# A graph layer on one core: spare products on zeros in the first unit, the weights' split moved off GpSimd, and one branch's columns copied out a unit earlier

## The reference

```python
def cxin_conv(x, a, eps, W, b):
    ax = a @ x
    h = ax + (1.0 + eps[0]) * ax
    for i in range(3):
        h = relu(h @ W[i].T + b[i])
    return h

h = maximum(layernorm(x), 0.0)
out1 = cxin_conv(h,  adj, eps1, W1, b1)
out2 = cxin_conv(x2, adj, eps2, W2, b2)
result = x + concatenate((out1, out2), axis=1) @ Wm.T + bm
```

## Time and profile before

| | |
|---|---|
| median of 3 runs | 415.06 us (414.89 to 415.40) |
| the profiled execution's own time | 414.96 us |
| its span, first to last instruction | 413.1 us |
| PE, busy | 404.5 us, 98% of the span, 1747 products |
| DVE, busy | 220.4 us, 53% |
| ACT, busy | 218.9 us, 53% |
| POOL, busy | 34.1 us, 8% |
| mean granted TensorE clock | 0.995 of full |

### The profile page before, as it was taken

One profiled execution on the slowest core, in us unless ns is written; L12 is line 12 of the kernel. 1 busy time (PEld: TensorE's weight loads), 2 busy tenths in 40 slices (PEclk: granted clock), 3 DMA queues, 4 the chain that ended last, 5 costly groups with the idle time before them and its releaser, 6 DMA issues.

```text
span 413.1 us, 4963 instructions
## 1 busy us (share of the span) xinstructions
PE 404.5 (98%) x1747; PEld 326.8 (79%) x1747; DVE 220.4 (53%) x274; ACT 218.9 (53%) x271; POOL 34.1 (8%) x37
## 2 busy tenths in 40 slices
PE   7999989999999999999999999999999999999996
PEld 2887768888888888888888888888888888888884
DVE  5899975452834456434555426455273454755222
ACT  5888892355543354553435554335554335765032
POOL 1443460000100000000100001000010000000100
PEclk9899999999999999999999999999999999999999
DMA  7998568432755508355293444843265541740100
GB/s 254 396 411 314 203 225 309 188 122 98 254 203 203 195 33 287 144 203 203 80 332 109 152 191 149 308 160 130 116 236 221 203 176 52 267 167 1 52 0 25
DMA packets 14745, 76.15 MB, mean 184 GB/s; under 512 B 2000, under 2 KB 2256, under 8 KB 6928
## 3 DMA queue, kind: packets, MB, share of 16 engines
q1 hardware_dynamic: 13392, 71.97, 46.8%
q0 software_dynamic: 1200, 3.93, 2.8%
q10 hardware_dynamic: 144, 0.13, 0.1%
HBM read 73.93 MB, written 2.10 MB: 184 GB/s over the span
## 4 chain that ended last, share of the span: by engine, by line
PE 85%; DVE 6%; ACT 5%; issue 2%; DMA 1%; SPq 1%; ACTq 0%; DVEq 0%
PE acc L429 25%; PE acc L433 25%; PE acc L430 25%; DVE adj_lo L386 3%; PE hidden L430 3%; PE hidden L429 3%; PE hidden L433 2%; ACT adj_hi L257 2%; DMA adj_raw<-adj_tiles 1%; DVE stats L354 1%; PE merged L430 1%; PE merged L429 1%; PE merged L433 1%; ACT x_rows L274 1%; DVE var_eps L359 1%
## 5 line engine op out<-in xcount | busy, mean ns | idle before, releaser
L429 PE MATMUL acc<-adj_hi,feat_lo 128*128 128x512 f32 x448 | 175.0, 391 | 1.6 <-ACT act_f L241 1.6
L433 PE MATMUL acc<-adj_lo,feat_hi 128*128 128x512 f32 x448 | 174.8, 390 | 0.0
L430 PE MATMUL acc<-adj_hi,feat_hi 128*128 128x512 f32 x448 | 174.3, 389 | 0.0
L330 DVE TENSOR_TENSOR adj_lo<-adj_raw,adj_hi 128x2048 fp32r<-128x2048 f32 x56 | 128.2, 2327 | 26.7 <-ACT adj_hi L224 26.7
L336 DVE TENSOR_TENSOR act_lo<-act_f,act_hi 128x512 fp32r<-128x512 f32 x60 | 41.4, 691 | 124.7 <-ACT act_f L241 124.7
L224 ACT ACTIVATE adj_hi<-adj_raw 128x2048 fp32r<-128x2048 f32 x56 | 104.8, 1930 | 2.2 <-PE acc L433 2.0
L429 PEld LDWEIGHTS acc<-adj_hi,feat_lo 128*128 128x128 f32 x448 | 84.1, 188 | 19.6 <-issue 2.0
L240 ACT ACTIVATE act_hi<-hidden,bias 128x512 fp32r<-128x512 f32 x45 | 31.0, 688 | 129.1 <-PE hidden L433 129.1
L433 PEld LDWEIGHTS acc<-adj_lo,feat_hi 128*128 128x128 f32 x448 | 84.1, 188 | 18.2
L430 PEld LDWEIGHTS acc<-adj_hi,feat_hi 128*128 128x128 f32 x448 | 84.1, 188 | 18.0
L240 ACT ACTIVATE act_hi<-acc,ax_scale 128x512 fp32r<-128x512 f32 x15 | 10.3, 688 | 44.7 <-PE acc L433 44.7
(11 more groups left out here) (60 smaller groups left out, 200.5 us busy)
## 6 DMA issues: line engine op xcount, KB each, us to landing
adj_raw<-adj_tiles SPq DMA_DIRECT2D x61, 1024.0 KB, 5.1
x_rows<-x_tiles SPq DMA_DIRECT2D x16, 256.0 KB, 6.4
adj_raw<-adj_tiles SPq DMA_DIRECT2D x12, 256.0 KB, 6.2
x_res<-x_t POOLq DMA_DIRECT2D x8, 256.0 KB, 6.2
out_t<-y_sb POOLq DMA_DIRECT2D x7, 256.0 KB, 2.3
w_raw<-w_t SPq DMA_DIRECT2D x1, 512.0 KB, 9.0
out_t<-y_sb SPq DMA_DIRECT2D x1, 128.0 KB, 1.8
out_t<-y_sb ACTq DMA_DIRECT2D x1, 128.0 KB, 1.9
```

Source lines behind the costliest of these rows:

```text
L330: nc.vector.tensor_tensor(adj_lo[:, u % RING, :], adj_raw[:, u % RING, :], f32(adj_hi[:, u % RING, :]), ALU.subtract).then_inc(lo_made, 1)
L429: nc.tensor.matmul(out, lhs_lo, rhs_hi, start=start, stop=False)
L430: nc.tensor.matmul(out, lhs_hi, rhs_hi, start=False, stop=False)
L433: return nc.tensor.matmul(out, lhs_hi, rhs_lo, start=False, stop=stop)
```

## The change

There are three parts. PE gets three more products on zeros at its start (`WARM_UP` 15), and two more (`FILLERS`) behind each of the four high x high products of unit 0 of branch 1. The weights are loaded three units earlier in SP's queue, split on ACT (`w_hi`, behind unit 5's features) and on DVE (`w_lo`, behind the last `adj_lo` of the first chunk), and POOL no longer touches them. The copies of step 0 are taken apart: branch 1's stand behind unit 0 of the next chunk, branch 0's behind unit 1 as before.

```diff
-    WARM_UP = 12
+    WARM_UP = 15
+    FILLERS = 2
+    WEIGHTS_AT = U - 3
-    OPERAND_AFTER = {1: 0, 3: 1, 5: 2, 7: 3}
+    OPERAND_AFTER = {0: ((0, BRANCH_ORDER[0]),), 1: ((0, BRANCH_ORDER[1]),),
+                     **{u: tuple((k, b) for b in BRANCH_ORDER) for u, k in {3: 1, 5: 2, 7: 3}.items()}}
-    LAST_OPERAND_AFTER = {1: 0, 3: 1, 4: 2, 5: 3}
+    LAST_OPERAND_AFTER = {0: ((0, BRANCH_ORDER[0]),), 1: ((0, BRANCH_ORDER[1]),),
+                          **{u: tuple((k, b) for b in BRANCH_ORDER) for u, k in {3: 1, 4: 2, 5: 3}.items()}}
...
-                if u == U - 2:
+                if u == WEIGHTS_AT - 2:
                     sp.dma_start(w_raw[:, :, :], w_t).then_inc(w_loaded, 16)
...
-            pool.wait_ge(w_loaded, 16)
-            nc.gpsimd.tensor_copy(w_hi[:, :, :], w_raw[:, :, :]).then_inc(w_hi_made, 1)
-            pool.wait_ge(w_hi_made, 1)
-            nc.gpsimd.tensor_tensor(w_lo[:, :, :], w_raw[:, :, :], f32(w_hi[:, :, :]),
-                                    ALU.subtract).then_inc(w_lo_made, 1)
             pool.dma_start(x_res[:, :], x_t[:, 0:CW]).then_inc(res_loaded, 16)
...
                 rectify(u)
+                if u == WEIGHTS_AT:
+                    act.wait_ge(w_loaded, 16)
+                    nc.scalar.activation(w_hi[:, :, :], w_raw[:, :, :], ACT.Copy).then_inc(w_hi_made, 1)
             act.wait_ge(bias_loaded, 16)
             act.wait_ge(scale_made, 1)
...
                 for j in range(JB):
                     fine_low(u, j)
+            dve.wait_ge(w_hi_made, 1)
+            nc.vector.tensor_tensor(w_lo[:, :, :], w_raw[:, :, :], f32(w_hi[:, :, :]),
+                                    ALU.subtract).then_inc(w_lo_made, 1)
             dve.wait_ge(eps_loaded, 16)
             dve.wait_ge(bias_loaded, 16)
...
+            def idle_products(n):
+                for _ in range(n):
+                    nc.tensor.matmul(merged[:, :], zeros[:, 0:P], zeros[:, :], start=True, stop=True)
...
                     nc.tensor.matmul(acc[b][:, :], feat_hi[:, b, u * JB + j, :], adj_hi[:, s, cols],
                                      start=(u == 0 and j == 0), stop=False)
+                    if fine and u == 0:
+                        idle_products(FILLERS)
```

More of the change, by code:

```diff
@@ L241, in branch_operand @@
                 nc.scalar.activation(act_f[:, b, :], src[:, :], **how).then_inc(act_f_made[b], 1)
-            def operand(m, k):
-                for b in BRANCH_ORDER:
-                    branch_operand(m, k, b)
             def fine_high(u, j):
@@ L294, in _ @@
                     high_of_unit(c, u)
-                    if u in OPERAND_AFTER:
-                        operand(c - 1, OPERAND_AFTER[u])
+                    for k, b in OPERAND_AFTER.get(u, ()):
+                        branch_operand(c - 1, k, b)
             for u in range(U):
                 high_of_unit(LAST, u)
-                if u in LAST_OPERAND_AFTER:
-                    operand(LAST - 1, LAST_OPERAND_AFTER[u])
+                for k, b in LAST_OPERAND_AFTER.get(u, ()):
+                    branch_operand(LAST - 1, k, b)
             for k in range(STEPS):
@@ L337, in low_of_branch @@
                                         ALU.subtract).then_inc(act_lo_made[b], 1)
-            def low_of_operand(m, k):
-                for b in BRANCH_ORDER:
-                    low_of_branch(m, k, b)
             def result(m):
@@ L402, in _ @@
                     low_of_unit(c, u)
-                    if u in OPERAND_AFTER:
-                        low_of_operand(c - 1, OPERAND_AFTER[u])
+                    for k, b in OPERAND_AFTER.get(u, ()):
+                        low_of_branch(c - 1, k, b)
                 result(c - 1)
@@ L407, in _ @@
                 low_of_unit(LAST, u)
-                if u in LAST_OPERAND_AFTER:
-                    low_of_operand(LAST - 1, LAST_OPERAND_AFTER[u])
+                for k, b in LAST_OPERAND_AFTER.get(u, ()):
+                    low_of_branch(LAST - 1, k, b)
             result(LAST - 1)
@@ L536, in _ @@
             pe.wait_ge(zeros_made, 1)
-            for _ in range(WARM_UP):
-                nc.tensor.matmul(merged[:, :], zeros[:, 0:P], zeros[:, :], start=True, stop=True)
+            idle_products(WARM_UP)
             for u in range(U):
```

## The result

The changed kernel takes 416.92 us (416.50 to 418.92, 6 runs), against 415.19 us in the same comparison: 1.0042 of the time before, 95% interval 1.0027 to 1.0057. It is 1.7 us slower. The forecast was 416.15 with a range up to 416.7, so the direction was right and the range too short by 0.2 us.

The account below looks back on a forecast made before the run. Feeding engines, through ACT's chain, bound the time before 58 us, PE's products the rest. Products on zeros 0, weights with earlier copies +1.15, on 414.96: 416.1, or 416.15 by the median; range 414.8 to 416.7.

Parts of the forecast that it names:

- Part 1, the products on zeros: Unit 0 on PE: up to 1.6 us sooner or 2.7 later, absorbed by the feeders before 58 us; 0.
- Part 2, the weights: First chunk's end: `w_lo` delays POOL and `ax_scale`, so ACT's loop and the third product; +1.15 us with the earlier copies.
- its cover: ACT's 0.91 us idle for `var_eps` absorbs `w_hi`; bounds 0 to 0.25 us, taken as 0.
- POOL ahead of DVE's next instruction: Behind `w_lo`, waiting POOL runs `feat_lo` first, to about 54.7; `ax_scale` ends at 54.75 instead of 52.40.
- Part 3, the earlier copies: Start of chunk 1: a gain of 1.1 us, taken by the late `ax_scale`; later chunks 0.
- The sum's +1.15: Chunk 1's third product at 59.45 instead of 58.32, +1.1, plus at most 0.1 for clearing after idle.
- 414.96 + 1.15: Whole kernel: the profiled execution's time plus the net loss gives 416.1; 416.15 by the median, 0.10 higher.
- the clock falls at the chunk's edge: PE's idle stretches before chunk 1's first products drop the clock: 1.6 us on top, 417.8; chance 0.06.

Follow-up runs that it names:

- fill_only: Kernel before with only the spare products on zeros added (`WARM_UP` 15, `FILLERS` 2 in unit 0): 415.77 us, ratio 1.0005.
- scale_first_nofill: Changed kernel with `ax_scale` ahead of `w_lo` on DVE and no spare products (`WARM_UP` 12, `FILLERS` 0): 414.30 us, ratio 0.9973 to before.
- copy_only: Kernel before with only branch 1's copies moved behind unit 0, weights still on POOL: 414.25 us, ratio 0.9973.
- before_again: Kernel before, no edit, run once more for a second profile: 415.43 us, ratio 0.9998.
- weights_fill: Changed kernel with both branches' copies behind unit 1 as before, spare products kept: 419.33 us, ratio 1.0089 to before.
- cold_start: Kernel before with one product on zeros at the start instead of 12 (`WARM_UP` 1): 415.42 us, ratio 0.9994.

## Why the prediction was wrong, step by step

**Part 1, the products on zeros: right.** Worth 0 by fill_only and scale_first_nofill within what the runs can tell, although the clock did what they were there for. The marks say why: PE is through unit 0's first branch a microsecond sooner or later and the rest stays the same, since the feeders set the pace of the first chunk.

**Part 2, the weights: right in each piece.** `w_hi` 1.05 against 1.06, its cover sufficient; `w_lo` 1.22 as worked out; POOL ahead of DVE's next instruction; POOL's subtraction 1.89 where about 2.0 was said, `ax_scale` 1.24 where 1.4 was, held to 0.03 behind POOL; 0.34 from its end to `adj_hi`, not 0.30; 2.05 and 2.29 behind that. From the row where `w_lo` starts to the third product is 7.12 us in the trace, and 7.22 in the working.

**Part 3, the earlier copies: right.** 1.1 us gained alone (copy_only), and lost whole to the late `ax_scale`. The later chunks paid 0.1 at most.

**The sum's +1.15: nearly right.** 1.08 by the rest in the profiles, 1.2 by the ten runs of the changed kernel at full clock against the 415.4 of before. (On the median of 415.06 it would give 416.21, not the 416.15 written; this changes nothing.)

**What 1.15 was added to: this is the step that failed.** "414.96 + 1.15", with `w_lo` from 52.23, takes the time at which the first chunk gets going from one profile and puts its difference between executions at nothing, without a reason. There rectifying started at 9.26, the earliest of all 13 profiles. In the profile of the changed kernel it started at 10.08, and `w_lo` at 53.06. These 0.82 us and the 1.08 of the mechanism are together the whole 1.9 between the two spans (413.1, 415.0). This execution took 416.89 at a mean clock of 0.999, so it lies outside the range with no fall of the clock. So does the median of the five runs at full clock in that comparison, again 416.89. The same program can do this alone: before_again started 0.97 later than its first profile. The base also came out higher with more runs, at 415.36 to 415.64 in the later comparisons, 0.3 to 0.6 above the 415.06 that I had. With ten runs at full clock the changed kernel lies 1.2 above it, not 1.7. So about 0.5 of the 1.73 is the luck of which executions were compared, as far as the runs show; up to some 0.2 of a late start by the spare products is not excluded.

**The rival "the clock falls at the chunk's edge": right price, wrong chance.** 1.6 worked out, 1.58 and 1.61 in the profiles. But I gave it 0.06, and it happened in 5 of 15 runs. I had also treated it as an alternative that a kernel shows or doesn't. It differs between executions of one kernel, so it belongs in the sum as a share: a third of 1.6 moves a mean by 0.5. A median moves less, from 416.6 to 416.89 over the 15 runs. In the six runs of the result it happened once, and without that run the median is 416.89 instead of 416.92: it isn't what carried the time out of the range. The evidence that I held against it was one row, the 1.60 us of idle at 57.74 at full clock; the changed kernel has three idle stretches there of together 2.7 us (0.77, 1.42 and 0.47, where 0.9, 1.4 and 0.8 had been worked out). The rule of the Trainium skill that I had beside it (TensorE: Matmul & The Clock Gate, HAM oscillation) tells of longer waits than these. The trace agrees with it in weights_fill (3.18 us, 5 of 5) and, of the changed kernel's runs, in a third. The same page (Part 1: The HAM clock gate) says that the gate's timing is not tied to the kernel's start, which would make it differ between executions as seen here; no run tests that.

## What to carry to other kernels

Before calling an engine's gap free, list what is queued behind the new instruction and who waits for that: here a two-number constant behind 1.2 us of work held up another engine's whole loop, and exchanging two statements turned 1.7 us lost into 1.3 gained (by the profiles, 1.1 lost into 1.1 gained); a POOL instruction that is already waiting takes its whole turn ahead of it. Take more than one profile for the base: a start that differs by 1 us between executions of one program is as large as the effect here. Subtracting it in each profile showed the effect to 0.1 us. If part of a cost depends on the clock at an idle stretch, put it into the forecast as a share of the runs.

## What was not expected of the hardware

The mark behind the first 256 KB transfers differs by 0.97 us between two executions of identical code (9.26 and 10.23), and by 1.5 us over all 13 profiles. The span follows one for one: the rest in the table stays within 0.1 us for kernels alike at the edge and in the clock there.

The profile's granted clock says 1.00 until its first recorded change. In cold_start it says 1.00 at 10 to 11 us, where the products go 0.43 us apart, the pace of 1.2 GHz. The distance between products tells more than that column at the start of a kernel.
